# Smaller row tiles in two mixture-of-experts stages: 384 rows in place of 512

## The reference

```
# block 0 (L = 0), F = 352
h = gelu(x @ w1[e]) * (x @ v1[e]);  y = h @ w2[e];  out = sum over 2 choices of weight * y + bias
# block 1 (L = 1), F = 512
h = gelu(x @ Wi[e] + bi[e]) * sigmoid(x @ Wg[e] + bg[e])
y = layernorm(x + h @ Wo[e] + bo[e]) * gamma[e] + beta[e];  out = sum over 2 choices of weight * y
```

## Time and profile before

| what | value |
|---|---|
| median of 3 runs | 1095.15 us (1092.53 to 1098.74) |
| profiled execution | 1095.04 us, of which its span is 1092.9 us |
| PE busy in the span | 962.0 us (88%) |
| DVE, ACT, POOL busy | 78%, 57%, 53% |
| granted TensorE clock, mean | 0.924 |
| HBM read and written | 106.71 MB and 63.76 MB |
| mixture of block 0, first turn to last | 462.8 to 621.7 us |
| mixture of block 1, first turn to last | 827.1 to 1037.9 us |

### The profile page before, as it was taken

One profiled execution on the slowest core, in us unless ns is written; L12 is line 12 of the kernel. 1 busy time (PEld: TensorE's weight loads), 2 busy tenths in 40 slices (PEclk: granted clock), 3 DMA queues, 4 the chain that ended last, 5 costly groups with the idle time before them and its releaser, 6 DMA issues.

```text
span 1092.9 us, 18047 instructions
## 1 busy us (share of the span) xinstructions
PE 962.0 (88%) x5608; PEld 629.6 (58%) x5608; DVE 851.3 (78%) x1897; ACT 618.4 (57%) x1248; POOL 578.8 (53%) x644
## 2 busy tenths in 40 slices
PE   5689999999999999899999937989886999999950
PEld 4443344343433434388888827556555888888850
DVE  7559999999999998155555547889892999999975
ACT  6118888788887888633333326223324667766642
POOL 7220588554344340035555546388881577667770
PEclk9559999999999999999999965799997999999985
DMA  6736657355454531246666561152213677777628
GB/s 209 304 105 200 194 155 227 114 164 176 130 171 131 174 105 38 87 149 204 182 205 201 167 154 39 41 182 71 64 39 94 194 191 224 207 212 224 209 68 236
DMA packets 121521, 170.37 MB, mean 156 GB/s; under 512 B 18801, under 2 KB 80594, under 8 KB 118354
## 3 DMA queue, kind: packets, MB, share of 16 engines
q1 hardware_dynamic: 94290, 110.94, 35.3%
q0 software_dynamic: 18688, 54.08, 14.5%
q10 hardware_dynamic: 8448, 4.20, 1.5%
HBM read 106.71 MB, written 63.76 MB: 156 GB/s over the span
## 4 chain that ended last, share of the span: by engine, by line
PE 69%; DVE 9%; issue 7%; POOL 6%; DMA 5%; ACT 3%; SPq 0%; ACTq 0%; POOLq 0%; DVEq 0%
PE ps L1168 13%; PE ps L1022 10%; PE ps L1123 10%; PE ps L324 8%; PE ps L326 7%; PE ps L325 7%; PE ps L1028 4%; POOL slots_x L797 3%; DVE nmax L1667 3%; PE ps L1141 2%; DMA stage<-token_y 2%; PE ps L1066 2%; ACT stage L1297 2%; DMA slots_x<-stage 2%; POOL stage L374 1%
## 5 line engine op out<-in xcount | busy, mean ns | idle before, releaser
L1667 DVE TENSOR_REDUCE nmax<-ps 128x1 f32<-128x512 f32 x512 | 324.3, 681 | 36.8 <-PE ps L1028 32.3
L1297 ACT ACTIVATE stage<-ps 128x512 f32<-128x512 f32 x512 | 274.4, 594 | 61.0 <-PE ps L1022 54.5
L841 POOL DMA_INDIRECT token_y<-stage,ids_now x184 | 181.5, 987 | 133.4 <-DVE stage L1723 57.0
L1028 PE MATMUL ps<-stage,stage 32*128 32x512 f32 x512 | 183.9, 504 | 15.0 <-DVE nmax L1667 13.8
L1022 PE MATMUL ps<-stage,stage 32*128 32x512 f32 x512 | 167.0, 480 | 8.6 <-ACT stage L1297 6.8
L1168 PEld LDWEIGHTS ps<-stage,stage 128*128 128x128 f32 (+1 forms) x1288 | 164.8, 191 | 13.8 <-DVE stage L1791 2.2
L1168 PE MATMUL ps<-stage,stage 128*128 128x128 f32 (+1 forms) x1288 | 171.3, 276 | 1.4 <-DVE stage L1791 1.2
L797 POOL DMA_INDIRECT slots_x<-xn,pos x128 | 138.3, 1081 | 38.9 <-issue 37.1
L1022 PEld LDWEIGHTS ps<-stage,stage 32*128 32x128 f32 x512 | 68.2, 181 | 148.5 <-ACT stage L1297 121.8
L324 PE MATMUL ps<-stage,stage 128*128 128x512 f32 x322 | 141.0, 438 | 3.6 <-issue 3.6
L1123 PE MATMUL ps<-stage,stage 128*32 128x512 f32 x1024 | 136.4, 605 | 0.0
(11 more groups left out here) (226 smaller groups left out, 1553.4 us busy)
## 6 DMA issues: line engine op xcount, KB each, us to landing
stage<-halves_w SPq DMA_DIRECT2D x23, 1024.0 KB
stage<-halves_w SPq DMA_DIRECT2D x23, 704.0 KB
stage<-slots_x SPq DMA_DIRECT2D x46, 260.0 KB
stage<-q_halves SPq DMA_DIRECT2D x32, 256.0 KB
halves_w<-stage POOLq DMA_DIRECT2D x16, 512.0 KB
k_halves<-stage SPq DMA_DIRECT2D x24, 256.0 KB
q_halves<-stage SPq DMA_DIRECT2D x24, 256.0 KB
stage<-k_halves SPq DMA_DIRECT2D x128, 48.0 KB
```

The costliest lines, as they stand in the source:

```text
L841: pool.indirect_dma_start(out=token_y, out_offset=bass.IndirectOffsetOnAxis(ap=ids_now[:, r, q:q + 1], axis=0), in_=ysb[:, r, q, :], in_of ...
L1028: pe.matmul(ps[:, (0, 1, 7)[bank_of(i)], :], head_rows(Qs, g2, j2)[:, t * P:(t + 1) * P], head_rows(Ks, g2, j2), start=True, stop=True).th ...
L1297: act.activation(probs[:, t % 2, j, :], ps[:, 2 + bank_of(i), :], ACT.Exp, scale=SCALE).then_inc(exp_set, 1)
L1667: dve.tensor_reduce(nmax[:, g % 2, at:at + 1], ps[:, (0, 1, 7)[bank_of(i)], :], AX, ALU.max, negate=True).then_inc(max_set, 1)
```

## The change

The tile becomes 384 rows, three blocks of 128, and there are 29 of them. All loops over the four blocks of a tile become loops over `KT = 3`, the counts that semaphores are waited for follow, tensors shrink, and fillers (`take`) keep the addresses of what lies behind them. The counting of an expert's tiles compares with `FULL = 11` thresholds in place of 8, since an expert can have 4096 rows. The order of the work on each engine stays: on POOL the scatters before `root` are still two, and one is left behind it.

```
-TILE = 512
-TILES = 23
+TILE = 384
+TILES = 29
+KT = TILE // P
+FULL = -(-SEQS * SEQ // TILE)
...
-        thr = sb("thr", [P, EXPERTS])
+        thr = sb("thr", [P, FULL])
+        over = sb("over", [P, EXPERTS, FULL])
...
-                link(dve.tensor_tensor(cmp8[:, :, :], spread(off[:, :], 2, E3), spread(thr[:, :], 1, E3), ALU.is_gt))
-                link(dve.tensor_reduce(ntile[:, :], cmp8[:, :, :], AX, ALU.add))
+                link(dve.tensor_tensor(over[:, :, :], spread(off[:, :], 2, O3), spread(thr[:, :], 1, O3), ALU.is_gt))
+                link(dve.tensor_reduce(ntile[:, :], over[:, :, :], AX, ALU.add))
...
-                    for q in range(4):
+                    for q in range(KT):
                         mm = pe.transpose(ps[:, 0, q * P:(q + 1) * P], xg[:, r, q, 0:D], ident[:, :])
...
-                        split3(pe, ps[0:M, bank + 2 * par, :], wu[:, r, 0, c], wu[:, r, 1, c],
+                        split3(pe, ps[0:M, bank + 2 * par, 0:TILE], wu[:, r, 0, c], wu[:, r, 1, c],
                                gT_hi[:, r, :], gT_lo[:, r, :]).then_inc(done[L], 1)
...
-                        scatter(i - 2, r, range(2, 4))
+                        scatter(i - 2, r, range(2, KT))
...
-                            weighted(i - 2, r, (2 * f, 2 * f + 1))
+                            weighted(i - 2, r, range(2 * f, min(2 * f + 2, KT)))
```

More of the change, by code:

```diff
@@ L826, in rows_of_tile, with scatter @@
                     if not (isinstance(i, int) and i < 2):
-                        pool.wait_ge(y_stored[L][r], (i - r) * 32)
+                        pool.wait_ge(y_stored[L][r], (i - r) * (8 * KT))
                     pool.tensor_copy(ids_now[:, r, :], ids[:, i, :] if isinstance(i, int) else
                                      ids[:, bass.ds(i, 1), :].rearrange("p a q -> p (a q)")).then_inc(ids_now_set[L], 1)
-                def scatter(i, r, part=range(4)):
+                def scatter(i, r, part=range(KT)):
                     if 0 in part:
@@ L859, in experts @@
                     rows_of_tile(TILES - 1, 0)
-                    scatter(TILES - 2, 1, range(2, 4))
+                    scatter(TILES - 2, 1, range(2, KT))
                     scatter(TILES - 1, 0)
@@ L1166, in down @@
                             pe.wait_ge(y_read[L], i - 1)
-                    for q in range(4):
+                    for q in range(KT):
                         mm = pe.matmul(ps[:, 5 + r, q * P:(q + 1) * P], hT[0:M, par, q * P:(q + 1) * P],
-                                       wdn[0:M, r, f, :], start=(f == 0 and q == 0), stop=(f == last and q == 3),
+                                       wdn[0:M, r, f, :], start=(f == 0 and q == 0), stop=(f == last and q == KT - 1),
                                        skip_group_check=True)
@@ L1720, in weighted @@
                     if not (isinstance(i, int) and i < 2):
-                        dve.wait_ge(y_stored[L][r], (i - r) * 32)
-                    for q in range(4):
+                        dve.wait_ge(y_stored[L][r], (i - r) * (8 * KT))
+                    for q in range(KT):
                         ins = dve.scalar_tensor_tensor(ysb[:, r, q, :], ps[:, 5 + r, q * P:(q + 1) * P],
@@ L1761, in center @@
                     dve.wait_ge(vec_in[r], (k + 1) * 32)
-                    dve.wait_ge(est_chain, i * 10 + 10)
-                    for q in range(4):
+                    dve.wait_ge(est_chain, i * CHAIN + KT + 6)
+                    for q in range(KT):
                         ins = dve.scalar_tensor_tensor(y[:, q, :], y[:, q, :], emean[:, q:q + 1], vecs[:, r, 0, :],
```

68 lines of the change are left out of this document (35 added, 33 removed).

## The result

The changed kernel takes 1114.36 us, the median of 4 runs (1110.43 to 1125.73). The kernel before took 1096.95 beside it (4 runs, 1092.53 to 1106.38). The ratio is 1.0170, with a 95% interval of 1.0116 to 1.0224: slower, by 1.2 to 2.2%. The prediction was faster, 1087.7, with a range that ended at 1101. Some executions take over 1.5% more than the fastest of their kernel by a disturbance that comes with any kernel; those are in the medians but not in the ratios, and the two profiles that fell on one (e9_after_again, e12_all_three) are not compared with others.

The account below looks back on a forecast made before the run. PE was taken as full in both mixtures, with block 1 paced by loops of DVE, POOL and loads. Block 0 -6.4, block 1 +3.9, the rest -4.8 sum to -7.3 from 1095.04: 1087.7 us, range 1074 to 1101.

Parts of the forecast that it names:

- Matmuls of 384 columns: On PE in both mixtures: matmuls 0.175 us apart, a tile 5.57 us in block 0 and 7.31 in block 1.
- Block 0 and the rest ahead of block 1: Block 0's PE time -6.4, its fewer scatters and weighting -1.6, filling `slots_x` -0.9, counting tiles +0.3 us.
- Behind PE's end: After PE ends in block 1, POOL issues four scatters in a row instead of six: -2.6 us.
- DVE and POOL in block 1: Loop from chunk 0 through scatters and `add_bias`, which holds `normalize`: 9.68 us a tile before, 7.45 after.
- Block 1, the loads: Two-tile loop from `normalize` through SP's load of `ebcol` to chunk 0: 7.8 us a tile, +3.9 us in all.
- Loads late in both stages: Rival: block 0's row loads late, 1095.8, or block 1 landings of 4.9 us, 1096.8; chance 0.19.
- The slow rival: Rival: DMA queueing in block 1 stretches `ebcol`'s landing, 13 us per us; at 6 us 1111; chance 0.14.
- PE's pace: Rival: both mixtures at PE's pace, block 1 at 7.4 us a tile, -17.4 in all, 1077.6 us; chance 0.25.
- The lock: Block 1's DVE and POOL: one waits for all of the other, but rows 5 and 6 contradict whichever-starts-first; no separate price.

Follow-up runs that it names:

- e9_after_again: The changed 384-row kernel run again with no further edit, on another chip: 1116.90 us, ratio 1.0159 to the kernel before.
- e12_all_three: 384-row kernel with `bo_row` on its own semaphore, `normalize` ahead of `add_bias`, gamma and beta loaded last: 1094.70 us, ratio 0.9965.
- e10_loads_light_again: The same kernel as e5_loads_light, run again on another chip: 1107.23 us, ratio 1.0051.
- e5_loads_light: 384-row kernel with `bo_row` on its own semaphore, half of block 1's up weights loaded from its third tile, gamma and beta last: 1111.85 us, ratio 1.0128.
- e1_bo_apart: 384-row kernel with `bo_row` on a semaphore of its own, so the turn waits for the tile's rows alone: 1092.69 us, ratio 0.9960.
- e6_loads_light_norm_first: The kernel of e5_loads_light with POOL's `add_bias` waiting until `normalize` of two tiles back is done: 1094.03 us, ratio 0.9974.
- e14_all_three_again: The same kernel as e12_all_three, run again on another chip: 1094.92 us, ratio 0.9927.

## Why the prediction was wrong, point by point

**Matmuls of 384 columns: right.** Up matmuls come 0.175 us apart (in block 0 they start at 541.84, 542.02, 542.20; those of 967.51 on, shown above, are at the lower clock), and a tile of block 0 without stops takes 5.49 where the sum gave 5.57.

**Block 0 and the rest ahead of block 1: right in sum, here.** Forecast were -6.4, -1.6, -0.9 and +0.3, together -8.6; block 1's first turn came 6.8 us earlier. Of the terms the -0.9 for the filling of `slots_x` isn't to be seen: block 0's first turn is at 463.0, before at 462.8. The loss that the prediction allowed for, up to 0.3 us a tile if a load lands late, exists in size (5.83 against 5.49) but from the stop on DVE and not from a load.

**Behind PE's end: right.** -2.6 forecast, -3.0 measured.

**DVE and POOL in block 1: the right loop, priced too low.** It was put at 7.45 us, and with no load in the way it was 7.8 (e10_loads_light_again, e5_loads_light), and 7.92 for the tile shown, so that 0.36 us a tile, 10 us over the block, were missing. `normalize` was held in 24 tiles of e1_bo_apart and 22 of e10_loads_light_again; in the changed kernel in 13, where the loads set the pace.

**"Block 1, the loads": the step that failed.** It names one loop over two tiles, through `ebcol`, prices it at 7.8 us a tile and takes 26 x 7.8. Two loads further down the same row of work on SP stands `bo_row`, and the turn waits for it. That loop is 8.66 us. 26 x (8.70 - 7.8) = 23.4 us, of the 26.7 by which the time was missed. Three parts made it: the issue is 4.18 us behind gamma and not 2.65; the landing is 5.8 us, where `ebcol`'s is 4.05 (4.2 in the sum); and four of the waits of PE brought 3.4 us each at half clock. The first two could be read in the kernel before, where `bo_row` is issued 4.2 us behind gamma as well (median) and landed in 4.5 to 5.3 us where a turn waited for it. The prediction looked at a load close ahead of its turn only for block 0, under "Loads late in both stages", and took its price there as a third of a us a tile.

**The slow rival** had the right mechanism (a landing stretched by what shares the queues) and nearly the right time, 1111, at the wrong load, with 0.14. Its argument against itself, that no transfer that grows stands ahead of `ebcol` in its queue, left out what stands behind. That its time comes near the measured 1114 is luck: it prices a landing of `ebcol` of 6 us, and that landing was 4.1.

**PE's pace** as a rival was 7.4 us a tile and 1077.6. PE's own work is what the sum says: behind the first two turns the shortest distances of e6_loads_light_norm_first and e14_all_three_again are 7.22 and 7.24, the sum has 7.31. The time was never reached all the same. The profiled execution of e14_all_three_again took 1097.56, 20.0 more than the rival has. Of these, block 0's turns are 28 x (5.83 - 5.57) = 7.3, block 1's 28 x (7.57 - 7.4) = 4.8, and the longer end behind the last turn 5.5, an estimate from the 15 and 20 us above. So the 5.4% fewer rows do make PE's work less, and small waits, the last tile's and block 0's stops, eat it.

**The lock, once more.** The Trainium skill ("SBUF — State Buffer", SBUF: two separate sides) gives the shared ports to whichever operation starts first, for its whole length. The prediction had rows 5 and 6 against it. The changed kernel's DVE has a hidden chunk in the same place:

```profile
907.39 1.69 DVE L1798 SCALAR_TENSOR_TENSOR stage<-stage,stage 128x384 f32<-128x384 f32 x1 [0.38 <-issue]
```
```profile
907.68 0.97 POOL L818 TENSOR_TENSOR stage<-stage,stage 128x384 f32<-128x384 f32 x1
```

DVE's operation began 0.29 us ahead of POOL's, takes 0.56 elsewhere, and ended 0.43 behind it, while POOL's took its usual 0.97. By the rule POOL would have been the one to wait. The trace does not agree, unless an operation's recorded start comes before it takes the ports, which no run here tells.

## What to carry to other kernels

When tiles get smaller, list for every wait of every engine the loop that closes over it, in tiles, with the fixed terms that don't shrink (issue, landing); a loop that was just short of binding binds next. Two loads on one semaphore cost the later one to whoever needs only the first; here one separate semaphore brought 17 us in block 1, 1.5%. What the further edits add to that in time is not known, since none of these kernels ran on the chip of e1_bo_apart; in block 1 they brought up to 11 us more. And look at the last tile as well: an order of loads that is better in the steady tiles can be worse there. Work removed from a full engine is a gain only if the time per tile falls as far as the number of tiles rises: 29 tiles have to turn in under 23/29 of the old distance, 5.7 us in block 0 and 7.6 in block 1; e14_all_three_again has 5.83 and 7.57.

## What the runs showed of the hardware that was not expected

- A load of 512 bytes to each of 128 partitions, issued ahead of 1 MB on the same queue, landed in 5.8 us (median); ahead of 0.5 MB, in 4.2. One issued 2.2 to 2.8 us ahead of the weights (medians) landed in 4.1 with either.
- Waits of PE of 1.97, 2.40, 2.54 and 2.85 us were each followed by 3.4 us at the lower clock level, matmuls of 384 columns 0.32 us apart in place of 0.175; one of 2.69 us was not.
- An operation of VectorE with two SBUF inputs that began 0.29 us ahead of one of GpSimd took 1.69 us in place of 0.56.
- In one execution the granted clock was 0.64 to 0.76 in stages in which PE was as busy as always (18.35 of 20 us in 80 to 100, in the changed kernel 18.38), and 1.00 in another of the same kernel.
